# Clears and first loads placed elsewhere in an attention and routed-experts block, and gathers six steps behind their pages

## The reference, cut to what matters

```python
# 1. token mixing: causal filter of 32 taps (rows padded in front), then two matrices
s = conv(pad(x, 32 rows), decay_w)              # (32, 376, 256)
h = (s @ Wv.T + bv * sum(decay_w)) @ Wo.T + bo
# 2. causal attention, 16 heads of 16
h = h + attention(layernorm(h)) @ wo + bo
# 3. two shared experts for every token, and 2 of 16 routed experts
flat = layernorm(h).reshape(-1, 256)            # 12032 tokens
probs = softmax(flat @ router_w)
weights, indices = top_k(probs, 2); weights /= weights.sum() + 1e-9
out = h + shared(flat) + sum_e comb[:, e] * ((silu(flat @ wg_r[e]) * (flat @ wu_r[e])) @ wd_r[e])
```

## Time and profile before

| | |
|---|---|
| median of 3 runs | 2238.45 us (2234.03 to 2239.76) |
| profiled execution | 2239.85 us |
| its span, first to last instruction | 2238.1 us |
| mean granted TensorE clock | 0.92 |
| TensorE busy | 1903.4 us, 85% |
| VectorE busy | 1395.3 us, 62% |
| ScalarE busy | 971.0 us, 43% |
| GpSimd busy | 958.6 us, 43% |

### The profile page before, as it was taken

The page is one execution under the profiler, slowest core; times in us unless marked ns, Lnnn a source line. Parts: engine busy times, 40 slices in busy tenths (PEclk is TensorE's granted clock), DMA queues, the critical chain, the costliest instruction groups (busy, mean ns, idle before and its releaser), DMA issues. The chain is left out here.

```text
span 2238.1 us, 49086 instructions
## 1 busy us (share of the span) xinstructions
PE 1903.4 (85%) x14417; PEld 1404.2 (63%) x14418; DVE 1395.3 (62%) x3805; ACT 971.0 (43%) x2062; POOL 958.6 (43%) x1315
## 2 busy tenths in 40 slices
PE   3899999999999999999999983978888858777773
PEld 3677777777777777777777652554455538766762
DVE  3467877878777777878778744555555532443433
ACT  1155565656566565656556552222222204332331
POOL 3034444444343444444344442555545432555455
PEclk7699999999999999999999975999999979888887
DMA  2233333334333333334333325222222126877775
GB/s 58 71 110 135 123 129 122 129 117 140 111 122 130 124 130 121 132 115 136 117 122 124 115 87 128 91 87 85 85 81 92 62 94 191 256 237 237 248 239 168
DMA packets 214514, 291.08 MB, mean 130 GB/s; under 512 B 44854, under 2 KB 176666, under 8 KB 214426
## 3 DMA queue, kind: packets, MB, share of 16 engines
q1 hardware_dynamic: 168634, 183.07, 26.3%
q0 software_dynamic: 18048, 49.31, 7.1%
q10 hardware_dynamic: 27744, 57.68, 6.9%
HBM read 83.25 MB, written 129.69 MB: 95 GB/s over the span
## 5 line engine op out<-in xcount | busy, mean ns | idle before, releaser
L797 DVE TENSOR_REDUCE neg_max<-bank 120x1 f32<-120x376 f32 (+2 forms) x896 | 526.3, 597 | 258.8 <-PE bank L589 248.1
L722 ACT ACTIVATE probs<-bank 128x376 f32<-128x376 f32 (+2 forms) x896 | 454.3, 522 | 305.9 <-PE bank L607 299.7
L575 PE MATMUL bank<-k_rows,q_rows 64*128 64x128 f32 (+2 forms) x1536 | 427.4, 350 | 50.2 <-DVE neg_max L797 27.6
L607 PE MATMUL bank<-q_rows,k_rows 64*120 64x120 f32 (+2 forms) x1536 | 392.4, 339 | 4.2 <-ACT probs L722 4.2
L575 PEld LDWEIGHTS bank<-k_rows,q_rows 64*128 64x128 f32 (+1 forms) x1536 | 238.3, 187 | 207.3 <-DVE neg_max L797 70.1
L908 POOL TENSOR_SCALAR_AFFINE_SELECT probs<-probs 128x512 f32<-128x512 f32 (+1 forms) x384 | 233.9, 628 | 282.6 <-ACT probs L722 282.6
L589 PE MATMUL bank<-causal,own_row 64*120 64x120 bf16 (+4 forms) x1792 | 277.5, 236 | 0.0
L2060 POOL DMA_INDIRECT y_got<-y_sorted,p_route x188 | 182.4, 970 | 212.1 <-DMA p_route<-route_dram 119.8
L1709 POOL DMA_INDIRECT x_sorted<-r_normed,route x188 | 183.7, 977 | 198.1 <-DVE route L1562 146.3
L607 PEld LDWEIGHTS bank<-q_rows,k_rows 64*128 64x128 f32 (+1 forms) x1536 | 223.3, 185 | 9.6 <-ACT probs L722 6.6
L643 PE MATMUL bank<-probs,val 128*32 128x376 f32 (+2 forms) x3072 | 194.7, 387 | 2.9 <-POOL probs L908 2.9
(11 more groups left out here) (204 smaller groups left out, 3811.3 us busy)
## 6 DMA issues: line engine op xcount, KB each, us to landing
x_sorted<-zeros ACTq DMA_DIRECT2D x32, 816.0 KB, 3.9
y_sorted<-zeros ACTq DMA_DIRECT2D x32, 816.0 KB, 4.5
x_rows<-x_sorted SPq DMA_DIRECT2D x51, 512.0 KB
y_sorted<-p_y_rows SPq DMA_DIRECT2D x51, 512.0 KB
q_rows<-q_flat_hi SPq DMA_DIRECT2D x256, 94.0 KB
k_rows<-k_flat_hi SPq DMA_DIRECT2D x256, 94.0 KB
q_rows<-q_flat_lo SPq DMA_DIRECT2D x128, 94.0 KB
k_rows<-k_flat_lo SPq DMA_DIRECT2D x128, 94.0 KB
```

What stands on the lines that cost most here:

```text
L575: eng.matmul(ps[0:T[t], m * w:(m + 1) * w], q[rows, slot, t * P:t * P + T[t]], k[rows, slot, 0:w], start=(m == 0), stop=False, skip_group_ ...
L607: last = eng.matmul(ps[0:T[t], m * w:(m + 1) * w], k[64 * c:64 * c + 64, slot, t * P:t * P + T[t]], q[64 * c:64 * c + 64, slot, t * P:S], ...
L722: eng.activation(probs[g % 2][0:T[t], first:first + len(heads), OFF[t]:OFF[t] + w], bank_exp[n % 2][0:T[t], 0:len(heads) * w].rearrange("k ...
L797: eng.tensor_reduce(dst, src, AX.X, ALU.max, negate=True).then_inc(max_taken, 1)
```

## The change

It moves four things. (1) `q_rows`, `k_rows` and `val` are cleared by GpSimd at the start of the attention block, each clear with a semaphore; SP waits for the four clears of rows before its first `rows`, VectorE for the two of `val` before its first `values`. (2) The x loads of batches 0 and 1 are issued by SP at the end of the setup. (3) `w_down_first` is cleared at the end of VectorE's routing step 0 and `w_down_second` at the end of step 1. (4) LAG is 6, so USED is 8: steps run from 0 to 54, and the loop from 12 to 43.

```diff
@@ setup, SP
                 eng.dma_start(bias_o[:, :], per_row(bo)).then_inc(late_loaded, 16)
+                full = P * (NT - 1)
+                for n in range(2):
+                    eng.dma_start(x_in[n][:, 0:NT - 1, :],
+                                  x[n, 0:full, :].rearrange("(t p) d -> p t d", p=P)).then_inc(x_loaded[n], 16)
+                    eng.dma_start(x_in[n][0:sh.T_in[-1], NT - 1, :], x[n, full:, :]).then_inc(x_loaded[n], 16)
@@ setup, GpSimd
                 eng.memset(moments[:, :, :], 1.0)
-                for p in range(2):
-                    eng.memset(val[p][:, :, :, :], 1.0)
-                    eng.memset(k_rows[p][:, :, :].bitcast(F32), 1.0)
-                    eng.memset(q_rows[p][:, :, :].bitcast(F32), 0.0)
@@ attention, VectorE, values
+                    if n == 0 and isinstance(st.i, int) and st.b == -1:
+                        eng.wait_ge(val_cleared, 2)
                     eng.wait_ge(dense_done, k + 1)
@@ attention, GpSimd, ahead of its steps
+                for p in range(2):
+                    eng.memset(k_rows[p][:, :, :].bitcast(F32), 1.0).then_inc(rows_cleared, 1)
+                    eng.memset(q_rows[p][:, :, :].bitcast(F32), 0.0).then_inc(rows_cleared, 1)
+                for p in range(2):
+                    eng.memset(val[p][:, :, :, :], 1.0).then_inc(val_cleared, 1)
@@ attention, SP, load_x
-                    for shift in (3, 4, 5) if st.b == FIRST else (5,):
+                    shift = 5
...
@@ attention, SP, rows
                         wait_alone(eng, dense_read, k + 1, passed_sp)
+                        if isinstance(st.i, int) and st.b == -2:
+                            eng.wait_ge(rows_cleared, 4)
@@ routing, VectorE
-                routed.clear(eng)
                 eng.wait_ge(r_consts, 1)
...
                         hidden_of(st, 1)
+                    if st.static and st.b in (0, 1):
+                        routed.clear(eng, st.b)
                 run_steps(eng, step)
@@ RoutedWeights
-    def clear(self, eng):
-        for n in range(2):
-            eng.memset(self.down[n][64 * (1 - n):64 * (1 - n) + 64, :, :], 0.0)
+    def clear(self, eng, n):
+        eng.memset(self.down[n][64 * (1 - n):64 * (1 - n) + 64, :, :], 0.0)
@@ pages
-    AHEAD, LAG = 5, 7
+    AHEAD, LAG = 5, 6
```

More of the change, by code:

```diff
@@ L165, in attention_phase @@
         x_loaded = [sem(f"x_loaded{p}") for p in range(2)]
+        rows_cleared = sem("rows_cleared")
+        val_cleared = sem("val_cleared")
         rows_loaded = [[sem(f"rows_loaded{p}_{h}") for h in range(2)] for p in range(2)]
@@ L980, in load_x @@
                 def load_x(st):
-                    for shift in (3, 4, 5) if st.b == FIRST else (5,):
[L983 to L994, removed]
+                    shift = 5
+                    if isinstance(st.i, int) and st.b + shift + 2 * st.i >= B:
+                        return
+                    par = (st.b + shift) % 2
+                    _, k = st.product("conv1")
+                    wait_alone(eng, dense_done, k + 1, passed_sp)
+                    n = st.b + shift + 2 * st.i
+                    full = P * (NT - 1)
+                    eng.dma_start(x_in[par][:, 0:NT - 1, :],
+                                  x[n, 0:full, :].rearrange("(t p) d -> p t d", p=P)).then_inc(x_loaded[par], 16)
+                    eng.dma_start(x_in[par][0:sh.T_in[-1], NT - 1, :], x[n, full:, :])\
+                        .then_inc(x_loaded[par], 16)
                 def rows(st, half, name):
```

## The result

| | before | after |
|---|---|---|
| median | 2239.11 us (2234.03 to 2244.46, 6 runs) | 2215.67 us (2210.46 to 2224.5, 6 runs) |
| profiled execution | 2239.85 us | 2213.07 us |
| its span | 2238.1 us | 2211.3 us |
| mean granted clock | 0.920 | 0.929 |

The account below looks back on a forecast made before the run. It took TensorE to bound attention, and waits to decide in routing and pages. Its terms, -5.0 + 2.3 - 2.3 + 1.0 = -4.0 us, gave 2234.4 us counted from the median of 2238.45, range 2227 to 2245.

Parts of the forecast that it names:

- -2.3 + 1.0 forecast: Pages: 2.3 us gained at the tail, 1 us charged because `combine` comes a step earlier while the gather hardly does.
- GpSimd waited 120 us for route loads: Pages: these waits were taken as mostly the page store still on its way, with GpSimd no bound.
- I took 4.0: Pages: 4.0 us assumed for a page store to land, between 0 and 4.6.
- The tail: End of the pages: gathers of batch 43 start at 2208.3 for 2210.61, 2.3 us gained; bounds 0 and 7.
- The third rival: Pages: VectorE's `combine` waits for gathers, +10 us in sum, 2248.5 us; chance 0.13.
- +2.3 forecast: Routing: clears moved to the ends of VectorE's steps 0 and 1 lose 2.3 us in sum; bounds 0 and 7.
- the earlier start: Start of routing: two clears of 3.47 us leave VectorE's start; gain costed at nothing, bounds 0 to 1.8 us.
- In step 1 the mechanism: Routing step 1: a 3.5 us clear delays `place` and so TensorE's router, against 1.2 us of slack: 2.3 us lost.
- There 3.5 us fit in on both: Routing step 2: VectorE idles 6.96 us before `gated`, TensorE 2.90 before `up`, so the clear loses nothing.
- an earlier issue gives nothing: Start of routing: the h2 load of group 2, issued 1.8 us earlier, still lies behind weights; nothing gained.
- -5.0 forecast: Setup and first attention steps: `var_eps` goes at 38.2 for 43.23, 5.0 us gained, kept through TensorE-bound attention.
- L342 freed: Setup: without GpSimd's clears the two `tensor_scalar` cost about 0.45 us for 5.40; what follows starts 4.9 us earlier.

Follow-up runs that it names:

- after_third: The changed kernel with nothing altered, run again in the session without holds: 2087.3 us, 1.0104 of the kernel before.
- gathers_in_pairs: The changed kernel with the gathers of two batches made together, eight in every second step, in the session without holds: 2084.21 us.
- same_rows: The changed kernel with its indirect reads using constant indices, the first 512 rows in order, in the session without holds: 2081.53 us.
- clears_in_wait2: The changed kernel with both clears of down weights at the end of VectorE's step -2, in the session without holds: 2072.31 us, 1.0027 of the kernel before.
- front_alone: The kernel before with only the change's setup and attention part (row clears and first x loads): 2233.6 us, 0.9970 of the kernel before.
- plain_on_gpsimd: The changed kernel with each indirect read replaced by a plain read of the same bytes on the same GpSimd queue: 2133.03 us.
- session E: A later measuring session, all kernels on one chip, with the holds; the kernel before took 2253.75 us.
- session D: The measuring session without holds, all kernels on one chip; the kernel before took 2067.19 us.

## Why the prediction was wrong

**The pages, -2.3 + 1.0 forecast, about -20 measured.** The step that failed is "GpSimd waited 120 us for route loads, but the page store issued just before them was mostly still on its way, and GpSimd is no bound there". With the route there, the first gather follows the store after 4.8 us in place of 8.6: the store was on its way for 4.8 us at most (I took 4.0), and 3.8 us of each batch's wait were the route's alone. And GpSimd bounds nothing by being waited for, but its gathers hold back TensorE's updates, some 100 us in sum, which no row I read showed as a wait on GpSimd: it stood as "remote" at the tanh and as a clock of 0.85. That the route load's place is worth the 20 us is shown; by what path, only argued (13 us of it by the clock). The tail, where I put the gain, gave 1.6 us: from the last y store's issue to the end 26.4 us before, 24.8 after.

**The third rival** (combine waits for gathers) did not come where it was forecast, 6.1 us in 360, I think because the holds stretch each step. Without holds it came, 84.3 us in 200.

**The clears of routing, +2.3 forecast, 6.3 to 7.0 measured, the earlier start's gain included.** In step 1 the mechanism was right and the size too small: a wait of 3.26 us, and the products behind it at half clock (3.76 us for 1.96). From router to router it was 21.2 us for 16.7. In step 2 the step that failed is "There 3.5 us fit in on both". Those idles stand at `gated` and `up`, behind the router; the clear stands ahead of it, where the row of before shows 0.67 us of slack. It cost 4.4 us again (20.7 for 16.3). The earlier start did give something: VectorE's `bn_stats` of group 2 came at 1387.43, 22.4 us into the stage for 23.9. Without holds the two clears cost 12 us (after_third, gathers_in_pairs and same_rows took 405.9, 403.5 and 403.0 us for routing, clears_in_wait2 392.3).

The page "DMA: Bandwidth & Descriptors" of the Trainium skill, section "Queues, rings and completion order", has a DMA engine take turns between queues by packet. The load of group 2 was issued 2.0 us earlier into the stage (13.07 us for 15.04) and its `bn_stats` came 1.5 us earlier, ahead of the landing of the last weights (22.4 us against 23.5), with packets of both queues side by side, 64 each from 1385 to 1386 us. That agrees with the rule. But its first packet came 6.1 us after its issue (5.4 in before; 1.0 for the loads of groups 0 and 4), so it did first stand behind weights, as I read from the packets. My conclusion, that an earlier issue gives nothing, was the wrong part.

**The front, -5.0 forecast.** The mechanism held, step by step: L342 freed, `var_eps` directly behind a clear of `val`. It came 6.9 us earlier, not 5.0. Of the 1.9 us more, 0.7 is chance: the first loads landed sooner (the reduction ahead of L342 at 7.44 for 8.16, and 7.11 to 8.16 in kernels with the old front too). Most of the rest is TensorE's, whose two groups of products in the setup (L312 and L315) took 4.34 us for 5.48, the last four 1.03 for 1.91; VectorE's rows there last as long in both. The 5.40 us of L342 are themselves one case of several: 3.8 to 9.6 us in the six traces with the clears in the setup, 0.73 in the fourteen without. In attention 5 us stayed (the h store at 1309.29 for 1314.52). At its end 2.1 were left: in the last static steps the clock was lower, for a reason that is open. Row of after, where before had 0.73 and 25.58 us of TensorE's work in the same stretch:

```profile
1320.00:1360.00 40.00, 27.34 (x149) 16.36 (x150) 10.47 (x22) 13.94 (x29) 14.59 (x19) 0.63 0.22 73
```

The kernel before starts routing at 1367.2 and 1368.5, four others with its front at 1369.3 to 1375.6, and the fourteen traces with the new front at 1362.1 to 1377.5. The means are 1371.2 and 1367.7: 3.5 us gained, less than executions differ by.

**The sum.** 2 to 6 gained in front, 6 to 7 lost in routing, 20 gained in pages: 15 to 20, where 21 to 23 were measured. The 20 is a mean: inside a session, single traces with the late and the early load differ in the pages by 6 to 34 us, the first two by 31. The range had its low end at 2227 because the pages were bounded by their tail, with nothing for the steps.

## What to carry to other kernels

A clear or copy put into an in-order engine costs its time less the slack of the next thing that others wait for, not of the longest idle found near it; and TensorE paid part of its wait again at a lower clock. Issue small loads that release a queue of work ahead of the large ones: here a load of 4 KB, issued 3.1 us (median of before) after the 512 KB store that it goes with and behind another load of 512 KB, cost 20 us where there were holds. When a wait has no releaser in the profile, compare the semaphore's time with the recorded end: the work may be done and its signal late. And look at how far apart late updates come: if they come faster than the work between them takes, the work was not what was late. A comparison should be made again in another session before a 1% gain is believed.

## What the runs showed of the hardware

- In all sessions but one, indirect transfers made by GpSimd held back the updates of TensorE's semaphores: up to 13.1 us at a time (front_alone), 86 to 112 us in sum over the pages of each kernel that has them. The products went on, and the updates came out 0.06 us apart. ScalarE, VectorE and GpSimd had no update over 0.1 us late in the pages. Plain transfers of the same bytes from the same queue held nothing (0 of 242 updates over 0.1 us late in plain_on_gpsimd). In routing it is alike with the scatters: ScalarE's wait at `logits` without a known releaser was 112.2 us in after from 1460 to 1700, and none in after_third, where a step took 14.3 us in the median for 18.5. The page "SBUF — State Buffer" of the Trainium skill, section "SBUF: two separate sides", says that only VectorE and GpSimd contend for a port and that TensorE waits for nobody. That is said of the ports to SBUF, and the holds are of updates, so they do not speak against it. No run here shows what the holds are made of.
- It is not so in every session: in one of six the same program took 2067 us for 2239 to 2255. What differs there is open. The record does not show that it is the chip, since session E, with the holds, has the chip number of session D. A change can win 1% with the holds and lose 1% without them.
- Two `tensor_scalar` of 128x128 took 0.73 us alone and 5.40 beside GpSimd's memsets: the first ended at 11.55 us and a memset at 11.48, the second at 14.17 and the next memset at 14.10. The same section says that GpSimd and some forms of VectorE instruction lock a shared port pair for a whole instruction, the later one waiting; these times agree.
